# A new table of steps, and one maximum instruction for a pair of heads

## The reference

```python
q, k, v = layernorm(x) @ Wq, context @ Wk, context @ Wv      # 8 heads of 64
attn = softmax(q k^T * 64**-0.5);  x = x + tanh(g_xattn) * ((attn v) @ Wo + bo)
probs = softmax(layernorm(x) @ router_weight.T); top 2 of 8 experts, capacity 1.25 * 2T / 8
x = x + tanh(g_ffn) * sum over the two experts of w * (pre * silu(gate)) @ post
```

## Time and profile before

| what | value |
| --- | --- |
| runs | 1834.96, 1835.0, 1838.59 us; median 1835.0 |
| profiled execution | 1836.31 us, its span 1834.6 us, mean granted clock 0.979 |
| PE busy | 1693.5 us, 92% |
| DVE busy | 1271.5 us, 69% |
| ACT busy | 1056.2 us, 58% |
| POOL busy | 679.0 us, 37% |

### The profile page before, as it was taken

How to read it: one execution, slowest core, us unless ns; L and a number is a source line. 1 busy time by engine, 2 the same in 40 slices (tenths; PEclk the granted TensorE clock), 3 DMA queues, 4 the chain that set the end, 5 groups by cost and what they waited for, 6 DMA issues and landing times. The chain is left out here.

```text
span 1834.6 us, 38501 instructions
## 1 busy us (share of the span) xinstructions
PE 1693.5 (92%) x13198; PEld 1538.1 (84%) x13199; DVE 1271.5 (69%) x2667; ACT 1056.2 (58%) x2229; POOL 679.0 (37%) x619
## 2 busy tenths in 40 slices
PE   5799999999999999999999997399999999999997
PEld 3688887887887887887888886299999999999997
DVE  4687887887888888887888876564554646546443
ACT  3667666666676676666676765154554545545443
POOL 3244345345345345345335333323233332333322
PEclk9899999999999999999999999599999999999999
DMA  6100001001001001001001011513323243231211
GB/s 188 36 1 24 14 22 49 15 22 48 13 24 48 13 24 48 13 24 48 13 24 36 20 40 60 180 24 104 93 35 98 29 104 92 33 99 29 33 26 28
DMA packets 65148, 85.89 MB, mean 47 GB/s; under 512 B 7208, under 2 KB 53800, under 8 KB 65008
## 3 DMA queue, kind: packets, MB, share of 16 engines
q1 hardware_dynamic: 47680, 64.08, 11.0%
q0 software_dynamic: 15984, 18.82, 5.9%
q10 hardware_dynamic: 1344, 1.20, 0.2%
HBM read 54.59 MB, written 29.48 MB: 46 GB/s over the span
## 5 line engine op out<-in xcount | busy, mean ns | idle before, releaser
L700 POOL TENSOR_SCALAR probs<-probs,row_rec 128x1024 f32<-128x1024 f32 x256 | 285.3, 1127 | 546.6 <-DVE row_rec L1526 530.2
L1065 ACT ACTIVATE pt_h<-turned 128x512 fp32r<-128x512 f32 x512 | 280.6, 601 | 244.2 <-PE turned L840 243.3
L1241 DVE TENSOR_TENSOR pt_l<-turned,pt_h 128x512 fp32r<-128x512 f32 x512 | 331.7, 681 | 19.0 <-ACT pt_h L1065 17.9
L1457 DVE TENSOR_REDUCE neg_max<-scores 128x1 f32<-128x1024 f32 x256 | 301.4, 1219 | 45.9 <-PE scores L828 45.0
L840 PEld LDWEIGHTS turned<-ident,probs 128*128 128x128 f32 x2048 | 226.4, 142 | 112.6 <-issue 49.9
L840 PE MATMUL turned<-ident,probs 128*128 128x128 f32 x2048 | 287.2, 281 | 36.0 <-DVE pt_l L1241 30.9
L1114 ACT ACTIVATE probs<-scores,neg_max 128x1024 f32<-128x1024 f32 x256 | 285.8, 1117 | 15.6 <-DVE neg_max L1457 15.4
L944 PE MATMUL ring<-pt_h,v_hl 128*128 128x256 f32 x1024 | 262.7, 294 | 7.9 <-DVE k_l L1241 5.3
L1693 DVE TENSOR_TENSOR act_f<-ffn,silu 128x256 f32<-128x256 f32 x288 | 122.2, 424 | 195.3 <-ACT silu L1195 181.9
L944 PE MATMUL ring<-pt_l,v_hl 128*128 128x256 f32 x1024 | 251.8, 283 | 0.0
L1195 ACT ACTIVATE silu<-ffn 128x256 f32<-128x256 f32 x288 | 110.7, 384 | 222.5 <-PE ffn L805 213.6
(11 more groups left out here) (221 smaller groups left out, 4064.7 us busy)
## 6 DMA issues: line engine op xcount, KB each, us to landing
w_raw<-w_t SPq DMA_DIRECT2D x16, 1024.0 KB, 5.7
e_rows<-lists SPq DMA_DIRECT2D x37, 260.0 KB, 2.7
ctx_raw<-ctx_t SPq DMA_DIRECT2D x16, 512.0 KB, 4.0
wg_raw<-wg_t SPq DMA_DIRECT2D x8, 1024.0 KB
lists<-rows SPq DMA_DIRECT2D x8, 520.0 KB, 7.9
x_in<-x SPq DMA_DIRECT2D x8, 512.0 KB, 4.9
x_sum<-x SPq DMA_DIRECT2D x8, 512.0 KB, 3.4
out<-x_sum SPq DMA_DIRECT2D x8, 512.0 KB, 3.0
```

What stands on the lines that cost most here:

```text
L700: nc.gpsimd.tensor_scalar(probs[:, k, :], probs[:, k, :], row_rec[:, k:k + 1], 1.0, ALU.mult, ALU.mult).then_inc(scaled, 1)
L1065: return nc.scalar.activation(dst, src, ACT.Copy)
L1241: return nc.vector.tensor_tensor(dst, src, hi_part.bitcast(F32), ALU.subtract)
L1457: nc.vector.tensor_reduce(neg_max[:, k:k + 1], scores[:, n % 2, :].rearrange("p (a c) -> p a c", a=2), AX.XY, ALU.max, negate=True).then_i ...
```

## The change

The table `JOBS` gives the jobs other steps, and the constants and special steps that go with it move along: work for the next batch starts at step 22, the pieces of the second layer norm one step earlier, POOL's steps by one or two, the second split of the weights in START from step 26 to 23. `highest` takes the maxima of both heads in one instruction, which reads 128x2048 and writes 128x2; it waits for both heads' scores, and `neg_done` counts pairs, so both exponentials wait for it.

```diff
 
 
 JOBS = {
-    0: [("v", 0, 3), ("w", 1, 0)],
-    1: [("w", 1, 1)],
-    2: [("k", 1, 0)],
-    3: [("v", 1, 0)],
-    4: [("k", 1, 1), ("q", 1, 0)],
-    5: [("w", 1, 2)],
-    7: [("w", 1, 3)],
-    8: [("v", 1, 1)],
-    9: [("v", 1, 2)],
-    10: [("k", 2, 0)],
-    11: [("k", 2, 1)],
-    12: [("v", 1, 3), ("q", 2, 0)],
-    14: [("h", 0, 0), ("h", 1, 0)],
-    16: [("w", 0, 0), ("w", 0, 1)],
-    18: [("q", 3, 0)],
+    0: [("w", 1, 0), ("k", 1, 0)],
+    2: [("w", 1, 1)],
+    3: [("k", 1, 1)],
+    4: [("w", 1, 2), ("q", 1, 0)],
+    6: [("w", 1, 3)],
+    7: [("v", 1, 0)],
+    8: [("v", 1, 1), ("k", 2, 0)],
+    10: [("k", 2, 1)],
+    12: [("h", 0, 0), ("v", 1, 2)],
+    13: [("q", 2, 0)],
+    14: [("v", 1, 3)],
+    15: [("q", 3, 0)],
+    16: [("h", 1, 0), ("w", 0, 0)],
+    18: [("w", 0, 1)],
     19: [("l", 0, 0)],
     20: [("k", 3, 0), ("w", 0, 2)],
-    22: [("k", 3, 1)],
-    23: [("x", 0, 0), ("x", 1, 0)],
-    24: [("w", 0, 3), ("q", 0, 0)],
-    26: [("v", 0, 0)],
-    27: [("r", 0, 0)],
-    28: [("k", 0, 0), ("k", 0, 1)],
-    29: [("v", 0, 1)],
-    31: [("v", 0, 2)],
+    21: [("k", 3, 1)],
+    22: [("x", 0, 0), ("x", 1, 0)],
+    23: [("v", 0, 0)],
+    24: [("w", 0, 3), ("k", 0, 0)],
+    27: [("q", 0, 0), ("r", 0, 0)],
+    28: [("k", 0, 1), ("v", 0, 1)],
+    29: [("v", 0, 2)],
+    30: [("v", 0, 3)],
 }
 LN_STEPS = 6
 GATE_STEPS = 27
 RANK_STEPS = 5
 CONSTS = 16
-NEXT_FROM = 23
+NEXT_FROM = 22
 SLOT_OF = {job: u for u, jobs in JOBS.items() for job in jobs}
 END_STEPS = 29
 
@@ -707,9 +706,9 @@
 
                         make_pads()
                     if body.prev:
-                        if u == 9:
+                        if u == 8:
                             power(1, b - 1)
-                        if u == 12:
+                        if u == 11:
 
                             pool.wait_ge(first_pads, 16 * E)
                             normalise(1, b - 1, x_sum, rows)
@@ -720,7 +719,7 @@
 
                             pool.wait_ge(listed, at(b - 1, 16 * 2 * QT, 16 * 2 * QT))
                             alone(pool)
-                    if body.own and u == 15:
+                    if body.own and u == 14:
 
                         pool.wait_ge(sum_loaded, at(b, 16, 16))
                         pool.wait_ge(bias_done, 1)
@@ -733,13 +732,13 @@
                             power(0, b + 1)
                         if u == 17:
                             normalise(0, b + 1, x_in, x_in)
-                        if u == 24:
+                        if u == 22:
                             if body.own:
 
                                 wait_filled(pool, body, max(body.where[job] for job in
                                                             (("k", 3, 1), ("v", 1, 3))))
                             split_ctx(b + 1, 0)
-                        if u == 26:
+                        if u == 24:
                             split_ctx(b + 1, 1)
                 if body is END:
                     for i in range(2 * QT):
@@ -1110,7 +1109,7 @@
             def exponent(b, n):
 
                 k = n % 4
-                act.wait_ge(neg_done, at(b, UNITS, n + 1))
+                act.wait_ge(neg_done, at(b, UNITS // 2, n // 2 + 1))
                 nc.scalar.activation(probs[:, k, :], scores[:, n % 2, :], ACT.Exp,
                                      bias=neg_max[:, k:k + 1], accum_out=row_sum[:, k:k + 1])\
                     .then_inc(exp_done, 1)
@@ -1142,7 +1141,7 @@
                         for i in range(3):
                             act.wait_ge(w_loaded[i], 16)
                             hi(w_h[0][i][:, :], w_raw[i][:, :]).then_inc(w_first_hi, 1)
-                    if body is START and u in (19, 26):
+                    if body is START and u in (19, 23):
 
                         flat = x_sum[:, :, :].rearrange("p q d -> p (q d)")
                         parts = (wq_h, probs[:, 0, :]), (wk_h, probs[:, 1, :]), (wv_h, flat)
@@ -1421,7 +1420,7 @@
                         v.wait_ge(tanh_done, 1)
                     if i == 1:
 
-                        v.wait_ge(neg_done, at(body.b, UNITS, 0))
+                        v.wait_ge(neg_done, at(body.b, UNITS // 2, 0))
 
                     wait_filled(v, body, c)
                     part = x_sum[:, j, :]
@@ -1453,10 +1452,9 @@
             def highest(b, n):
 
                 k = n % 4
-                v.wait_ge(scores_done, at(b, UNITS, n + 1))
-                nc.vector.tensor_reduce(
-                    neg_max[:, k:k + 1], scores[:, n % 2, :].rearrange("p (a c) -> p a c", a=2),
-                    AX.XY, ALU.max, negate=True).then_inc(neg_done, 1)
+                v.wait_ge(scores_done, at(b, UNITS, n + 2))
+                nc.vector.tensor_reduce(neg_max[:, k:k + 2], scores[:, :, :], AX.X, ALU.max,
+                                        negate=True).then_inc(neg_done, 1)
 
             def low_turned(b, n, j):
 
@@ -1470,7 +1468,7 @@
 
                 b = body.b
                 if body.prev:
-                    n = {(7, 4): 0, (8, 4): 1, (9, 0): 2, (9, 3): 3, (10, 4): 4, (11, 0): 5, (11, 2): 6, (11, 4): 7}.get((u, gap))
+                    n = {(6, 4): 0, (7, 4): 1, (8, 0): 2, (8, 3): 3, (9, 4): 4, (10, 0): 5, (10, 2): 6, (10, 4): 7}.get((u, gap))
                     if n is not None:
                         if n in (0, 1):
 
@@ -1517,7 +1515,6 @@
                     between(body, u, 0)
                     if body.own and u % 2 == 0:
                         highest(b, u)
-                        highest(b, u + 1)
                     between(body, u, 1)
                     if body.own and u % 2 == 1:
```

## The result

The changed kernel takes 1858.15 us (median of 4 runs, 1857.33 to 1858.58) against 1835.64 for the kernel before on the same chip: ratio 1.0123, 95% interval 1.0107 to 1.0138, slower by 22.5 us. The profiled execution spans 1856.2 us, 21.6 more than before. It was forecast at 1857. Among the later runs, one of the kernel before (2359.97 us, granted clock 0.656) and one of e6 (3141.08 us, 0.898) were far slower; the ratios leave them out, and they move the medians that they stand in by less than 0.3 us.

What follows compares the result with a forecast made beforehand. PE was taken as the bound, with small holes (busy 130.06 of 137.09 us in a loop batch). Terms 2.3 + 19.3 + 1.8 - 0.5 = +22.9 us gave 1858 on the median of 1835.0, rounded to 1857; range 1826 to 1871.

Steps and rivals of the forecast that it cites:

- End of the first batch: Start and first batch together: first S at about 32.0 instead of 34.31, later pairs longer, the end +2.3 us.
- with the exps late in the first pairs too: First batch's early pairs: late exponentials counted into the +2.3 us for its end, without a figure of their own.
- the gain of 3 at step 5: First batch: PE's 5.31 us wait for k_l behind wo's split shifts to the next turn, gaining about 3 us.
- Six loop batches: The six loop batches of the attention part: 844.4 against 825.06 us, +19.3; table gains 2.6 a batch, merge loses 6.4.
- the walk: Pair-by-pair estimate of a loop batch on the new table: 141.35 us with the merge, 134.9 with the old exp delays.
- Last batch and end: Last batch, without next-batch jobs: +1.8 us to step 28; w at 2 instead of 1 hides a drain, -0.5.
- Experts: The last 650 us or so of the kernel, same instructions before and after: 0 change.
- the delay is hidden and the table wins: Rival: exp's 0.75 us delay never reaches S or a bank, 134.9 us a loop batch, 1817 in all; chance 0.18.
- No single pass: Rival on DVE's merged maximum: it takes 2.44 us, a further 0.16 in some ten pairs, +13, 1870; chance 0.06.
- The clock falls: Rival: waits in pairs 12, 22 and 28 make PE's clock fall once a batch more, 1.6 us each, 1870; chance 0.08.
- the signs that I named: Profile signs: 128 merged maxima of 2.2 to 2.35 us, exp waits, exp u at 4.0, batches 140 to 142, S near 32.
- S waiting for ACT's probs: Sign in PE's waits: scores would wait for ACT's probs in pairs 10 and 26; no size given.

Runs made afterwards that it cites:

- e6: Changed kernel with two separate maxima, POOL's subtraction in four pieces, and at step 21 DVE's reciprocal and w's drain before the routing piece: 1824.82 us, ratio 0.9935.
- the first experiment: The changed kernel with the merge taken back: new table, one maximum per head, each exponential waiting for its own; 1824.70 us, ratio 0.9943 to the kernel before.
- e9: The new table with one maximum over both heads only in pairs 8, 12, 16, 20, 22 and 28, two maxima elsewhere: 1842.14 us, ratio 1.0034.
- e10: The new table with two maxima in pairs 8, 12, 16, 20, 22 and 28, one merged maximum in the other ten: 1840.11 us, ratio 1.0025.

## Why the prediction was right, and where its terms were not

The direction and the mechanism are as recorded; of the +22.9 us recorded for the span 21.6 came. Term by term, measured on the profiled executions:

- *End of the first batch*, +2.3 recorded: the first S 2.90 earlier, the batch 7.62 longer, +4.7. The start was right (v near 19.5 recorded, 18.50; first S 32.0, 31.41). The batch was under-estimated: with two maxima it takes 139.17, so 6.9 of the 7.6 us are the merge. Set against the first experiment pair by pair, pairs 0 and 8 pay 1.1 and 1.2 of the 6.9, pair 6 0.75, and the eleven from 10 on 4.1 together. From pair 10 on the batch is 4.7 longer than before, where +3.9 was recorded, so that term held roughly. The pairs in front of it are 3.0 longer, where the recorded terms leave about 0.7: the step "with the exps late in the first pairs too" had no figure of its own, and the gain of 3 at step 5 (5.31 in the earlier trace rows) moved elsewhere. Pair 4 is 7.4 shorter, pairs 6 and 8 are 5.7 and 2.3 longer: what takes the place of the wait is one of 6.2 us of o for v_hl in step 9, behind the split of wo (5.3 with two maxima), and one of 3.8 of a turn for POOL (the waits of the changed kernel between 31.41 and 177.52):
```profile
PE ring L943 <- DVE v_hl L1240: 6.2, 1, 6.2
...
PE turned L839 <- POOL probs L699: 3.8, 1, 3.8
```
- *Six loop batches*, +19.3 recorded, +13.1 measured. Two terms were mis-sized in opposite directions. The table alone was to gain 2.6 us a batch and gains (825.06 - 819.38) / 6 = 0.9. The merge was to cost 6.4 a batch and costs (838.16 - 819.38) / 6 = 3.1 on the new table, 5.0 on the old one.
- *Why the merge was too dear in the walk*: the delay itself was right (4.0 after S recorded, 4.05), and so was the maximum's 2.28 (2.287). Pair by pair, recorded and measured: 8 9.5 and 9.09, 20 10.5 and 10.26, 22 10.0 and 9.75, 28 11.5 and 10.74, 12 10.15 and 10.23, 10 7.2 and 6.94, 0 9.2 and 8.65 ("PE restarts at half clock" came true behind one of the changed kernel's five jumps, and behind two of the kernel before's). The walk had the maximum of pair 28 start 3.25 after S; it started at 2.36 (579.89). And of the 3.3 us a batch between recorded and measured price, 1.7 are no discount of the merge but pair 24's loss to the lock in the first experiment (10.09 in the mean of its six batches, 8.43 in the changed kernel). The lock goes by where the product lands, not by the merge in the pair itself: e9, with pair 22 merged and pair 24 not, takes 8.46 in pair 24, and e10, with pair 24 merged and pair 22 not, has one batch of six with 10.48 and the same 1.96 us product.
- *Why the table gained less*: pair 24, at 8.6 recorded, took 10.09 with two maxima, 1.65 more than where the product misses POOL (8.44). That is nearly all of the 2.6 - 0.9 = 1.7 us a batch. The profile before could not show it at that place, but it has the same kind of wait in pair 22. Beside it, l takes 1.8 us to the next S and not the 0.8 that I estimated without a row; pair 18 took 8.18 where 7.5 was recorded.
- *Last batch and end*, +1.8 and -0.5 recorded, +3.0 measured (191.1 - 188.1), made of -4.0 by the table and +7.0 by the merge. The pairs without jobs don't stand at a floor that both share: pair 22 takes 6.51 with two maxima and 7.00 with the merge. And 1.4 of the 7.0 are pair 24 (9.05 and 10.42), in which the clock fell in the changed kernel and not in the other:
```profile
1122.60:1126.00 3.40, 3.40 (x19) 3.17 (x17) 2.33 (x6) 0.93 (x2) 2.22 (x2) 0.50 0.02 5
```
  Experts: 0 recorded, +0.8.

Summed over the profiled executions, the table: -3.2 in the start, +0.7 in the first batch, -5.7, -4.0 and +0.7 behind, -11.6. The merge: +0.3, +6.9, +18.8, +7.0 and +0.1, +33.2. The recorded walk had six batches at 134.9 less 3.7 for the missing jumps without the merge, 805.7, so -19.4 for the table and +38.7 for the merge. The total was hit by luck: a merge over-charged in the loop by 20 met a table over-credited there by 14 and a first batch, a last batch and experts under-charged by 5. Not each step was right.

Of the rivals, "the delay is hidden and the table wins" fell: its 1817 would have needed a free delay, and the table with no delay at all gives 1824.7. "No single pass" fell with 2287 ns. "The clock falls", once a batch more, is out: the granted clock of the six loop batches is 0.99 to 1.00 in their windows, before and after; the one fall more that counts is that of the last batch, 1.4 us. The rule of the Trainium skill that spoke against the merge (Perfetto Trace Analysis, section Optimizing Scalar/DVE Operations) holds here, with its size now measured: 8.7 us of DVE saved, 33 to 42 us of time lost.

Of the signs that I named, four came out as said: 128 merged instructions of 2.29 us, exp idle before neg_max (103.2 us), exp u 4.05 after S, and the first S. S waiting for ACT's probs shows behind pair 10 alone, once a batch and by 0.3 (PE's weight load, 317 to 1015), and not behind 26:
```profile
PEld scores L827 <- ACT probs L1113: 1.6, 5, 0.3
```
The batches, 139.7 to 140.5 and the last, without a jump behind it, 138.0, lie at or under the lower edge of 140 to 142.

The version that beats both is the changed kernel with its two maxima back: 1824.70 us, and 1823.42 with POOL's pieces, 0.6% under the kernel before.

What stays open: why the granted clock falls behind some of the jumps and not behind others, what of the median's small differences between kernels that is, and which of the merged pairs hands what to which; no run merged a single pair.

## What to carry to other kernels

Before two instructions are merged, ask who starts on the first one's result. Here 8.7 us / 128 = 0.07 us a pair was saved and the consumer of the first half, the exponential, was put off by 0.8 us, on an engine that runs in order with drains behind it. A forecast by parts is only tested by the parts: the two edits here have opposite signs, and a total that agrees to 1 us said nothing about either until each ran alone. And slack that a pair hides from the bounding engine is not gone; look into the next pair's queue for it.

## What the runs showed of the hardware

A VectorE instruction of 128x32 with both inputs in SBUF took 1.96 us instead of 0.19 while a GpSimd instruction of 2.39 us ran, and ended 0.05 us behind it; one that met a GpSimd TENSOR_SCALAR of 1.05 us took 1.10 and ended 0.03 behind it, though it was recorded as started 0.02 us earlier. VectorE instructions that read PSUM between them kept their time. I had put no price on this: a tiny product took here up to ten times its 0.19 us, depending on what GpSimd instruction it met, and whether it met one changed from batch to batch (8.44 or 10.5 us for the same pair). Cut into four, the GpSimd instruction took 2.83 us instead of 2.39, and the second product took 0.31 at that place; the first still met the unsplit TENSOR_SCALAR and took 1.04 to 1.06.

A fall of the granted clock from 1.0 to 0.5 (the levels of 2.4 and 1.2 GHz) for about 3.4 us made one pair of steps 0.8 to 1.5 us longer (9.3 against 8.2 and 8.5 for pair 0 with two maxima, 12.04 against 10.5 for pair 24). PE had stood still before it, 1.52 us in that pair 24 and 2.6 us at such a jump of the loop, but the same waits also passed without a fall.
